# A CIN tower on one core: the low part of one chunk of squares made on GpSimd instead of VectorE

## What is computed

```python
def _cin_layer(x0, xk, W, b):
    out = jnp.einsum('bhd,bmd,shm->bsd', xk, x0, W) + b[None, :, None]
    return jax.nn.relu(out)
x1 = _cin_layer(x0, x0, W1, b1)          # W1: 128 x 39 x 39
x2 = _cin_layer(x0, x1, W2, b2)          # W2: 128 x 128 x 39
p1 = x1.sum(axis=-1)
p2 = x2.sum(axis=-1)
h = jnp.concatenate([p1, p2, dense_ctx], axis=1)   # then three dense layers
```

## Time and profile before

| | |
|---|---|
| three runs | 1169.5, 1169.6, 1169.92 us; median 1169.6 us |
| the profiled execution | 1168.95 us, with a span of 1167.2 us (1.75 us lie around the span) |
| granted TensorE clock, mean | 0.989 of full speed |
| PE busy | 1131.9 us (97%), 4973 matmuls recorded |
| DVE busy | 1077.7 us (92%), 3840 instructions |
| POOL busy | 896.6 us (77%), 930 instructions |
| POOL look-ups (line 461) | 320, 962 ns in the mean |
| POOL idle before its adds (line 470), waiting for ACT | 126.4 us |
| ACT busy | 697.9 us (60%), 2193 instructions |

### The profile page before, as it was taken

One profiled execution on the slowest core, in us unless ns is written; L12 is line 12 of the kernel. 1 busy time (PEld: TensorE's weight loads), 2 busy tenths in 40 slices (PEclk: granted clock), 3 DMA queues, 4 the chain that ended last, 5 costly groups with the idle time before them and its releaser, 6 DMA issues.

```text
span 1167.2 us, 19434 instructions
## 1 busy us (share of the span) xinstructions
PE 1131.9 (97%) x4973; PEld 913.2 (78%) x4973; DVE 1077.7 (92%) x3840; ACT 697.9 (60%) x2193; POOL 896.6 (77%) x930
## 2 busy tenths in 40 slices
PE   5499999999999999999999999999999999999998
PEld 3377787888887888888888777888888888888876
DVE  4378999999999999999999878999999999999976
ACT  4365666566765666676656556666666666666543
POOL 6488989888988888889888767888887555555532
PEclk9799999999999999999999999999999999999998
DMA  6101111111111111111111110111111000000000
GB/s 201 6 4 7 7 6 7 8 6 7 7 7 6 8 6 7 8 6 7 7 7 6 6 6 5 7 7 7 8 6 6 1 1 1 1 1 2 0 1 1
DMA packets 170381, 12.00 MB, mean 10 GB/s; under 512 B 163630, under 2 KB 169262, under 8 KB 170141
## 3 DMA queue, kind: packets, MB, share of 16 engines
q1 hardware_dynamic: 160029, 8.13, 7.8%
q0 software_dynamic: 10240, 2.64, 2.9%
HBM read 8.31 MB, written 0.00 MB: 7 GB/s over the span
## 4 chain that ended last, share of the span: by engine, by line
PE 89%; POOL 4%; DVE 2%; another core or an unknown queue 2%; issue 2%; ACT 1%; DMA 0%; POOLq 0%; SPq 0%; DVEq 0%; ACTq 0%
PE ps L995 23%; PE ps L996 23%; PE ps L999 23%; PE ps L931 4%; PE ps L959 3%; PE ps L960 3%; PE ps L962 3%; PE ps L1029 3%; DVE acc L860 2%; POOL looked L461 2%; POOL fy L470 2%; PE ps L923 1%; PE ps L964 1%; PE ps L1006 1%
## 5 line engine op out<-in xcount | busy, mean ns | idle before, releaser
L860 DVE SCALAR_TENSOR_TENSOR acc<-ps,e,acc 128x128 f32<-128x128 f32 x3186 | 850.9, 341 | 29.8 <-PE ps L999 25.3
L995 PE MATMUL ps<-w2h,x1h 128*128 128x512 f32 (+1 forms) x1280 | 507.4, 396 | 17.4 <-ACT x1h L638 15.3
L470 POOL TENSOR_TENSOR fy<-fy 128x512 f32<-128x512 f32 (+1 forms) x256 | 403.0, 1574 | 140.6 <-ACT fy L597 126.4
L996 PE MATMUL ps<-w2l,x1h 128*128 128x512 f32 (+1 forms) x1280 | 495.2, 387 | 0.0
L999 PE MATMUL ps<-w2h,x1l 128*128 128x512 f32 (+1 forms) x1280 | 493.2, 385 | 0.0
L597 ACT ACTIVATE fy<-ps,e 128x128 f32<-128x128 f32 x1536 | 415.4, 388 | 62.8 <-PE ps L999 60.8
L461 POOL DMA_INDIRECT looked<-in_table,rows x320 | 308.0, 962 | 68.4 <-issue 36.7
L995 PEld LDWEIGHTS ps<-w2h,x1h 128*128 128x128 f32 x1280 | 241.3, 188 | 76.2 <-ACT x1h L638 15.7
L999 PEld LDWEIGHTS ps<-w2h,x1l 128*128 128x128 f32 x1280 | 240.7, 188 | 48.2 <-DVE x1l L797 0.2
L996 PEld LDWEIGHTS ps<-w2l,x1h 128*128 128x128 f32 x1280 | 240.9, 188 | 47.9 <-issue 3.3
L624 ACT ACTIVATE zh<-ps 128x512 fp32r<-128x512 f32 x174 | 107.1, 616 | 195.0 <-PE ps L931 185.4
(11 more groups left out here) (104 smaller groups left out, 628.0 us busy)
## 6 DMA issues: line engine op xcount, KB each, us to landing
e<-looked SPq DMA_DIRECT2D x360, 5.0 KB, 1.9
looked<-in_table,rows POOLq DMA_INDIRECT x320
e<-looked SPq DMA_DIRECT2D x120, 4.5 KB, 1.9
w_st<-in_w SPq DMA_DIRECT2D x1, 1728.0 KB
wt_sb<-in_wt SPq DMA_DIRECT2D x2, 512.0 KB
w_st<-in_w SPq DMA_DIRECT2D x1, 768.0 KB
w_sb<-in_w1a SPq DMA_DIRECT2D x1, 448.0 KB
w1b_sb<-in_w1b SPq DMA_DIRECT2D x1, 448.0 KB
```

What stands on the lines that cost most here:

```text
L470: nc.gpsimd.tensor_tensor(out, a, b, ALU.add).then_inc(s_fsum, 1)
L860: nc.vector.scalar_tensor_tensor(acc[:, sub, :] if m < fields("D", last)[-1] else y, y, emb(p, sub, m), acc[:, sub, :] if m else fsum[:, p ...
L995: nc.tensor.matmul(y, x1h[:, t % 2, at], w2h[:, cols], start=True, stop=False)
L996: nc.tensor.matmul(y, x1h[:, t % 2, at], w2l[:, cols], start=False, stop=False)
```

## The change

The low part of chunk 3 is made by GpSimd for the tiles from 5 on (27 tiles). For these, ScalarE writes the whole square to the SBUF buffer `z1` and not back to PSUM; GpSimd subtracts `zh` from it into `zl`, in pair 2t - 3, between the look-up that follows `four_to_two(then, 2, 1, 0)` and `four_to_two(then, 3, 2, 8)`; TensorE waits for a semaphore of GpSimd's in front of the matmul with `zl`, and the next expansion into the bank BK_T waits for the squares and no longer for the low part. VectorE leaves that `square_low` out. The other five chunks stay as they were.

```diff
+POOL_CHUNK = 3
+def by_pool(t, v):
+    return t >= SOON and v == POOL_CHUNK
+def pool_splits(t, v):
+    return sum(by_pool(u, w) for u in range(t + 1) for w in range(C1) if (u, w) <= (t, v))
+def pool_split_in(p):
+    return next((t for s in range(SLOTS) for t, v in layer1_steps(p, s) if by_pool(t, v)), None)
+def lows(t, v):
+    return splits(t, v) - pool_splits(t, v)
@@ split_after
-    return [at for s in range(slots[j], slots[j + 1]) for at in layer1_steps(p, s) if is_split(*at)]
+    return [at for s in range(slots[j], slots[j + 1]) for at in layer1_steps(p, s) if is_split(*at) and not by_pool(*at)]
@@ GpSimd
+                def square_low(t):
+                    k = C1 * t + POOL_CHUNK
+                    pool.wait_ge(s_sq, splits(t, POOL_CHUNK))
+                    pool.wait_ge(s_mm1, k - 1)
+                    nc.gpsimd.tensor_tensor(zl[:, k % 2, :], z1[:, k % 2, :], zh[:, k % 2, :], ALU.subtract).then_inc(s_zl_pool, 1)
...
                         four_to_two(then, 2, 1, 0)
                     look_ahead(1)
+                    if (t := pool_split_in(p)) is not None:
+                        square_low(t)
                     if then < PAIRS:
                         four_to_two(then, 3, 2, 8)
@@ ScalarE, square
-                        nc.scalar.activation(src, src, ACT.Square).then_inc(s_sq, 1)
+                        whole = z1[:, k % 2, :] if by_pool(t, v) else src
+                        nc.scalar.activation(whole, src, ACT.Square).then_inc(s_sq, 1)
@@ TensorE, staging of the bank BK_T
-                            if is_split(*at):
-                                pe.wait_ge(s_zl, splits(*at))
+                            if by_pool(*at):
+                                pe.wait_ge(s_sq, splits(*at))
+                            elif is_split(*at):
+                                pe.wait_ge(s_zl, lows(*at))
@@ TensorE, layer1
-                        pe.wait_ge(s_zl, splits(t, v))
+                        if by_pool(t, v):
+                            pe.wait_ge(s_zl_pool, pool_splits(t, v))
+                        else:
+                            pe.wait_ge(s_zl, lows(t, v))
```

More of the change, by code:

```diff
@@ L354, in cin_tower @@
         s_zl = sem("s_zl")
+        s_zl_pool = sem("s_zl_pool")
         s_late = sem("s_late")
```

## The result

| | before | after | ratio (95% interval) |
|---|---|---|---|
| first chip | 1169.76 us | 1192.24 us | 1.0179 (1.0163 to 1.0195) |
| second chip | 1154.63 us | 1172.63 us | 1.0155 (1.0142 to 1.0169) |

The change makes the kernel slower: by 22.5 us on the first chip, by 18.0 us on the second, where 17.9 had been predicted. The measured 1192.24 us lies inside the stated range (1182 to 1195) and just outside the prediction's own narrower one (1184 to 1192). The profiled execution on the first chip took 1191.48 us with a span of 1189.7 us. For the second chip +19 to +19.5 us had been expected before that run, so its 18.0 is a little less.

A forecast was written before the change was run, and what follows sets the result against it. TensorE sets the pace at 33.50 us a tile; GpSimd, nearly full while issuing look-ups, becomes the limit. 14.4 + 4.1 - 0.6 = 17.9 us slower, median 1187.5 us; 8-in-10 range 1182 to 1195.

The forecast's parts named there:

- GpSimd's queue is the bound while look-ups go out: While issuing look-ups GpSimd has 0.2 to 0.3 us to spare in 33.5; with the change it needs 34.6 a tile.
- The price of one: One 128x512 subtraction on GpSimd adds 1.30 us to its queue, between 1.25 and 1.44; upper end 2.41 with fp32r output.
- Tile 5: At the first changed tile TensorE waits 2.9 us at once for zl, since GpSimd is already late there.
- To tile 18: Each earlier subtraction moves GpSimd's queue 1.30 us further; TensorE's zl load in tile 18 comes 14.4 us late in all.
- Tiles 19 to 21: Dense layers stretch TensorE's time to 117.61 us, GpSimd needs 103.8 and catches up; no further loss, tile 21 just in time.
- Tiles 22 to 25: Up to pair 47, the last with look-ups, GpSimd falls behind again: 4.1 us more.
- Tiles 26 to 31: With the look-ups gone, GpSimd's 4.47 us of idle time hides the subtraction; no loss.
- VectorE: 27 subtractions of 0.68 us removed, worth at most TensorE's waits of 4.7 us; 0.6 us taken off, around the dense layers.
- fsum: GpSimd's sum that VectorE waits for: 1.4 us to spare before the change, about 0.1 after; adds nothing.

The follow-up runs named there:

- The runs on the fourth chip: Two variants of the changed kernel: a second GpSimd subtraction into an unused buffer, 1218.62 us; the subtraction on GpSimd only from tile 9 on, 1186.56 us.

## Why the prediction was right

- **GpSimd's queue is the bound while look-ups go out.** Shown. More queue without a wait for zl costs the time (12.6 us), less queue with the wait gives it back (15 of 18 us, like with like), the same instruction past the look-ups costs nothing.
- **The price of one.** 1.294 us in the mean, against 1.30; the next add starts 1.24 us after it, the lower end of the range (1.25). fp32r output costs nothing extra. (The prediction's own range speaks of 17 subtractions; its sums hold 14 to tile 18 and 5 to tile 25, 19 in all, which makes that range about 17.0 to 20.6 us.)
- **Tile 5.** Predicted 2.9, measured 3.04 (6.96 - 3.92) between the lateness at tile 4 and at tile 5.
- **To tile 18.** Predicted 14.4 from the start, measured 19.18 - 3.92 = 15.3 on the first chip and 15.25 - 0.47 = 14.8 on the second. The price was a little too high in the sum (14 x 0.06, 0.8 us), and still the first chip lost 0.9 us more than predicted, so some 1.7 us have another source. VectorE's operations with two SBUF inputs held GpSimd 0.57 us longer than in the kernel before (last section), and one wait of 0.4 us for a field was left where the sum had none; the rest was not traced.
- **Tiles 19 to 21.** Predicted no loss, measured -0.1.
- **Tiles 22 to 25.** Predicted 4.1, measured 4.15.
- **Tiles 26 to 31.** Predicted nothing, measured -0.1. Behind tile 31 the first chip's traces win 0.5 us back and the second's lose 1.0; the stretch from that load to the end is 78.8 to 79.8 us in all traces and was not looked into.
- **VectorE.** The 0.6 us taken off for it did not come: the load of tile 21 is only 0.11 earlier against tile 18 than before. Its freed time turned into waiting for TensorE (11.7 us between 203 and 655 us). This is the one term of the sum that was wrong. Its cap was read short too: 4.7 us is one row of the waits for VectorE, and the rows of that view for weight loads come to 15.8 us from 176 us on, though by the same view of the matmuls they wait only 3.2 us for VectorE there.
- **fsum.** Predicted to be left about 0.1 us and to add nothing. In pair 10 the sum ends at 241.84 and VectorE starts from it at 241.94; the experiment one look-up earlier shows that this second bound stands right behind the first.
- **The size.** 18.0 us beside 17.9 is closer than the sum deserves. The price made the sum 1.1 us too high (19 x 0.06), while the 0.6 taken off for VectorE and the missing stops and wait of GpSimd's made it too low; and in the second chip's trace, which is 1.6 us longer than the median, the loads lose 18.6 us from tile 4 to 31. That the sum holds to about 1 us is borne out; the last tenths are luck.
- **The start.** 3.9 of the 22.5 us on the first chip are not the change's mechanism. The prediction had no term for it, and its range held them only because it was wide. The runs on the fourth chip, with the long start as well, have an excess of the same kind: 48.5 us in the medians where the loads lose 45.6 from tile 4 on, and 16.4 where they lose 14.4. With the short start there is none. So the new code may lengthen the long start by some 2 to 4 us; what sets the start stays open, and no experiment was made on it.

## What to carry to other kernels

Read an engine's room from the spacing of one of its instructions over many rounds, less its waits for data, and not from its busy share. GpSimd was busy 77% of the span. The window of the earlier trace rows gives it 85%, but reaches past the last look-up at 889 us; in front of that it is 89% (columns as in the earlier trace rows):

```profile
751.17:885.33 134.16, 134.16 (x606) 111.09 (x606) 133.19 (x478) 85.00 (x268) 119.36 (x125) 1.00 0.13 7
```

Even the 89% hid a queue with only 0.2 to 0.3 us to spare in 33.5: the small holes between GpSimd's instructions were no room for the new one, which lengthened the queue by its full 1.24 us. Taking work from an engine at 99% busy was worth next to nothing here, since another engine set the pace. Where a queue is too long, a better place in it helps once; shortening it helps every round.

## What the runs showed of the hardware

A VectorE operation with two SBUF inputs holds up the GpSimd instruction that starts while it runs, for most of the time that is left of it. In the changed kernel an add of 64 columns, 0.32 us elsewhere, took 1.18 us beside it:

```profile
362.22 1.26 DVE L822 TENSOR_TENSOR ctx_r<-ctx_sb,ctx_r 16x1024 fp32r<-16x1024 f32 x1
```

```profile
361.94 0.46 POOL L552 TENSOR_TENSOR xt<-xs 128x128 f32<-128x128 f32 x1
362.48 1.18 POOL L552 TENSOR_TENSOR xu<-xt 128x64 f32<-128x64 f32 x1
```

Of the 1.00 us that the two ran together the add lost 0.86. In the earlier trace rows it is 0.62 us of 0.75, in the kernel with the unused subtraction an add at 342.05 took 1.45 us instead of 0.46, and with the subtraction twice a look-up at 368.44 took 2.00 instead of 0.96. A GpSimd instruction that had started before VectorE's lost nothing: the add of 128 columns above took its usual 0.46, and in the kernel before a look-up from 386.87 to 387.83 took 0.96 beside a second such operation of VectorE's that started at 387.11. The Trainium skill (GPSIMD Engine Reference, section 8, Key points) names this contention for DVE instructions with two SBUF inputs; the trace agrees, and the steady operations, with one input from PSUM, leave GpSimd's adds at 1.30 us. In the changed kernel an add of 0.32 us, at 398.28, took 0.65 beside this second operation (397.93, 0.81 us). With a queue that is the bound, such a stop is lost time: 0.86 + 0.33 us in the changed kernel, 0.62 in the kernel before (1.58 - 0.96).

A GpSimd subtraction with the same tensor as both inputs took 1.05 us for 128x512 (27 in the mean), and one with two tensors 1.29.
